# Row factors of a graph attention: by DMA through DRAM instead of by transposes on PE

## The reference

```python
h = jnp.einsum('bmi,ih->bmh', x, Wp) + bp
scores = s_src[:, :, None] + s_dst[:, None, :]
scores = jnp.where(scores >= 0, scores, 0.2 * scores)
attn = jax.nn.softmax(jnp.where((A_final <= 0)[None], fill, scores), axis=-1)
h_gat = jnp.einsum('bmn,bnh->bmh', attn * A_final[None], h)
```

## Time and profile before

| | us |
|---|---|
| median of 2 runs | 1026.09 (1020.98 to 1031.19) |
| the profiled execution | 1025.88 |
| its span in the profile | 1024.1 |

### The profile page before, as it was taken

One profiled execution on the slowest core, in us unless ns is written; L12 is line 12 of the kernel. 1 busy time (PEld: TensorE's weight loads), 2 busy tenths in 40 slices (PEclk: granted clock), 3 DMA queues, 4 the chain that ended last, 5 costly groups with the idle time before them and its releaser, 6 DMA issues. The chain is left out here.

```text
span 1024.1 us, 21202 instructions
## 1 busy us (share of the span) xinstructions
PE 957.3 (93%) x7355; PEld 908.4 (89%) x7355; DVE 870.2 (85%) x2532; ACT 632.7 (62%) x1641; POOL 549.4 (54%) x1169
## 2 busy tenths in 40 slices
PE   6779999999999999999999999999999899997998
PEld 5679998998988899899989899999899899887897
DVE  5989797999989987978899889699989879779884
ACT  2446557686668653675575674777548584777741
POOL 3426254681786651755566464456727635467831
PEclk9878999999999998999999999999999999999999
DMA  7020000000020010002000101100000100000004
GB/s 141 2 62 2 1 2 1 2 2 1 2 83 2 2 42 2 1 21 63 2 1 1 43 1 42 43 2 22 22 1 2 42 2 2 1 1 2 1 1 124
DMA packets 38490, 20.17 MB, mean 20 GB/s; under 512 B 3184, under 2 KB 37872, under 8 KB 38384
## 3 DMA queue, kind: packets, MB, share of 16 engines
q1 hardware_dynamic: 36512, 18.42, 6.8%
q10 hardware_dynamic: 1872, 0.40, 0.2%
HBM read 10.43 MB, written 8.39 MB: 18 GB/s over the span
## 5 line engine op out<-in xcount | busy, mean ns | idle before, releaser
L639 PE MATMUL ps<-HE,PT 128*128 128x129 f32 x2048 | 241.0, 277 | 5.9 <-issue 2.3
L639 PEld LDWEIGHTS ps<-HE,PT 128*128 128x128 f32 x2048 | 234.8, 193 | 9.3 <-issue 8.6
L925 ACT ACTIVATE Y<-X,SM 128x128 f32<-128x128 f32 x512 | 203.9, 487 | 41.8 <-POOL SM L1083 41.7
L1068 POOL TENSOR_TENSOR SM<-ST 128x8 f32<-128x8 f32 x96 | 28.4, 296 | 294.9 <-DVE ST L1154 294.8
L1291 DVE SCALAR_TENSOR_TENSOR PT<-ps,CE,maskT 128x512 f32<-128x512 f32 x256 | 174.1, 742 | 13.7 <-PE ps L763 7.8
L1079 POOL TENSOR_TENSOR SM<-SM,minus_half 128x8 f32<-128x8 f32 x96 | 162.1, 1688 | 7.6
L639 PE MATMUL ps<-W,HT 128*128 128x128 f32 (+1 forms) x768 | 126.7, 312 | 0.7 <-issue 0.4
L639 PEld LDWEIGHTS ps<-W,HT 128*128 128x128 f32 x768 | 116.0, 193 | 10.1 <-ACT HT L918 0.6
L1154 DVE BATCH_NORM_STATS2 ST<-X 128x6 f32<-128x128 f32 x512 | 104.9, 277 | 3.2
L656 PE MATMUL ps<-ident,Y 128*128 128x128 f32 x640 | 86.5, 279 | 11.5 <-ACT Y L925 9.8
L656 PEld LDWEIGHTS ps<-ident,Y 128*128 128x128 f32 x640 | 72.5, 144 | 17.7 <-ACT Y L925 15.4
(11 more groups left out here) (262 smaller groups left out, 2348.9 us busy)
## 6 DMA issues: line engine op xcount, KB each, us to landing
X<-in_x_dram SPq DMA_DIRECT2D x32, 256.0 KB, 3.4
out_dram<-X SPq DMA_DIRECT2D x32, 256.0 KB, 2.8
adj_raw<-in_adj_dram SPq DMA_DIRECT2D x4, 256.0 KB, 3.7
W<-in_L_gnn_W_dram SPq DMA_DIRECT2D x1, 128.0 KB, 5.7
Ws<-n_L_gnn_self_weight_dram ACTq DMA_DIRECT2D x1, 64.0 KB, 3.1
W<-in_L_gnn_W_dram ACTq DMA_DIRECT2D x1, 64.0 KB, 3.5
feat2w<-in_L_gnn_W_dram ACTq DMA_DIRECT2D x1, 64.0 KB, 4.3
Wo<-L_gnn_others_weight_dram SPq DMA_DIRECT2D x1, 64.0 KB, 5.8
```

Source lines behind the costliest of these rows:

```text
L639: return nc.tensor.matmul(o, w, m, start=start, stop=stop, skip_group_check=True)
L925: a = A(dst[:, n, 0:F], src[:, n, 0:F], func, scale=SM[s][:, S_RSTD, n:n + 1], bias=SM[s][:, S_SHIFT, n:n + 1])
L1068: TT(sm[:, S_DIF, :], st[:, :, 1], st[:, :, 4], ALU.subtract)
```

## The change

1. The four steps `spread1a`, `spread1b`, `spread2a`, `spread2b` of PE go. In their place come `spill1`, `fill1`, `spill2`, `fill2` on SP: two DMAs write `CE`'s columns 8 to 15 (512 elements of 4 bytes each DMA) to a scratch in DRAM, and one DMA reads the 1024 factors back, 4 KB to each of the 128 partitions, into `HI[s]`. `fill` waits for the landing of `spill`.
2. The DVE step of the attention reads the row factors from `HI[s]` in SBUF instead of from PSUM, waits for `filled` instead of for the PSUM tile, and no longer waits for its own end.
3. The set-up block: `erank` (16 matmuls of 128 x 512 and four copies) moves from the edge work into it; 32 small matmuls with `cnt_row` give way to four that turn `off_b`; row counts come from ACT's accumulator instead of two DVE reductions; some copies go from DVE to ACT; loads are cut into three sets, with fewer broadcasts; for groups 0 and 1 (`EARLY`) the first layer norm's statistics, `rstd` and scaling are done there.
4. `TURNS` and `HOMES` are written anew, for all engines and all steps.

```diff
+EARLY = 2
-    ("spread1a", 1, "pe"),
-    ("spread1b", 1, "pe"),
+    ("spill1", 0, "sp"),
+    ("fill1", 0, "sp"),
...
 PREP = [
-    ("erank", 4, "pe act"),
...
+                def spill(u, name, s):
+                    n = ATT[name[-1]]
+                    sp.wait_ge(sig["dexp"][s], count(u.g, 4, 2 * n))
+                    for b in range(G):
+                        sp.dma_start(factors[s, n, b * N:(b + 1) * N].rearrange("(t p) -> p t", p=P),
+                                     CE[s][:, TG + b:2 * TG:G],
+                                     allow_slow_non_contiguous=True).then_inc(sig["spilled"][s], 16)
+
+                def fill(u, name, s):
+                    n = ATT[name[-1]]
+                    sp.wait_ge(sig["spilled"][s], count(u.g, 2, n) * 16 * G)
+                    sp.dma_start(HI[s][:].bitcast(F32).rearrange("p r f -> p (r f)"),
+                                 factors[s, n, :].partition_broadcast(P)).then_inc(sig["filled"][s], 16)
...
-                def spread(u, name, s, b):
-
-                    pe.wait_ge(sig["dexp"][s], count(u.g, 4, 2 * ATT[name[6]]))
-                    o, done = open_tile(u, name, s)
-                    for t in range(T):
-                        n = TG + t * G + b
-                        mm = T_(o[:, t * P:(t + 1) * P], wide(CE[s][:, n:n + 1]), ident[:])
-                    mm.then_inc(done, 1)
...
-                    o, read = filled(u, "spread" + name[3:], s)
+                    dve.wait_ge(sig["filled"][s], count(u.g, 2, n) * 16)
+                    o = HI[s][:].bitcast(F32).rearrange("p r f -> p (r f)")[:, b * N:(b + 1) * N]
                     for j in range(T):
                         c = j * G + b
                         a = V.scalar_tensor_tensor(out=PT[r][:, j, :], in0=o, scalar=CE[s][:, c:c + 1],
                                                    in1=maskT[:, j, :].bitcast(F32), op0=ALU.max, op1=ALU.mult)
                     a.then_inc(p_full[r], 1)
-                    dve.wait_ge(p_full[r], u.matrix(name)[1] + 1)
-                    dve.sem_inc(read, 1)
```

In the set-up block:

```diff
+                for i in range(T):
+                    for j in range(T):
+                        mm = MM(ps[i // 2][:, (i % 2) * N:(i % 2 + 1) * N], maskT[:, j, i * P:(i + 1) * P],
+                                upper[:, j, :], start=(j == 0), stop=(j == T - 1))
+                    if i % 2 == 1:
+                        mm.then_inc(made["rank"], 1)
...
+                for s in range(EARLY):
+                    if s == 1:
+                        act.wait_ge(made["rowtot"], 1)
+                        A(rowtot_b[:], ps[3][:, 0:N], ACT.Copy)
+                        for h in range(2):
+                            act.wait_ge(made["rank"], h + 1)
+                            A(rank[:, 2 * h:2 * h + 2, :], ps[h][:].rearrange("p (a n) -> p a n", a=2), ACT.Copy)
+                    act.wait_ge(sig["rstd"][s], 1)
+                    scaled(Y[s], X[s], s, ACT.Relu).then_inc(sig["normed"][s], 1)
```

More of the change, by code:

```diff
@@ L446, in _ @@
                     sp.sem_inc(s, 16)
[L447 removed]
+                sp.wait_ge(loaded["rest"], 16 * len(REST))
             @block.gpsimd
@@ L467, in _, with link @@
                 nc.gpsimd.iota(mc_int[:], [[P, MB]], base=0, channel_multiplier=1).then_inc(made["pool"], 1)
+                order = [0]
+                def link(ins):
+                    order[0] += 1
+                    ins.then_inc(pool_order, 1)
+                    pool.wait_ge(pool_order, order[0])
+                for s in range(EARLY):
+                    pool.wait_ge(sig["var"][s], 1)
+                    rstd_of(pool, link, s, False).then_inc(sig["rstd"][s], 1)
+                pool.wait_ge(loaded["rest"], 16 * len(REST))
+                nc.gpsimd.tensor_scalar(bias3[:], bias3[:], -1.0, None, ALU.add)
+                pool.sem_clear(pool_order)
             @block.tensor
@@ L506, in _ @@
                 MM(ps[2][:, 390:391], bprep[:], asum[:], start=True, stop=True).then_inc(made["wvec"], 1)
+                for i in range(T):
[4 more added lines that the diff above has]
+                        mm.then_inc(made["rank"], 1)
+                pe.wait_ge(made["off_b"], 1)
+                for i in range(T):
+                    mm = MM(ps[2][:, N + 400 + i:N + 401 + i], off_b[:, i * P:(i + 1) * P], ident[:, 0:1], start=True, stop=True)
+                mm.then_inc(made["off_col"], 1)
             @block.scalar
@@ L628, in store @@
                         sp.dma_start(rows_of(out, u, b), X[s][:, b::G, :]).then_inc(sig["stored"][s], 16)
-                walk("sp", {"load": load, "store": store})
+                def spill(u, name, s):
[10 more added lines that the diff above has]
+                                 factors[s, n, :].partition_broadcast(P)).then_inc(sig["filled"][s], 16)
+                walk("sp", {"load": load, "store": store,
+                            "spill1": lambda u, s: spill(u, "spill1", s), "fill1": lambda u, s: fill(u, "fill1", s),
+                            "spill2": lambda u, s: spill(u, "spill2", s), "fill2": lambda u, s: fill(u, "fill2", s)})
                 for s in range(NS):
@@ L810, in mlp @@
                         mm.then_inc(done, 1)
-                def erank(u, s):
-                    for i in range(T):
-                        o, done = open_tile(u, "erank", s, i)
-                        for j in range(T):
-                            mm = MM(o, maskT[:, j, i * P:(i + 1) * P], upper[:, j, :], j == 0, j == T - 1)
-                        mm.then_inc(done, 1)
                 def eoffm(u, s):
@@ L828, in eedge @@
                 def eedge(u, s):
-                    for i in range(T):
-                        turned(u, "erank", s, i)
                     for t, src in enumerate((adjn, rank)):
@@ L999, in feat3 @@
                         A(HI[s][:, t * G:(t + 1) * G, :], v[:, :, F:2 * F], ACT.Copy).then_inc(sig["hi"][s], 1)
-                def erank(u, s):
-                    for i in range(T):
-                        o, read = filled(u, "erank", s, i)
-                        A(rank[:, i, :], o, ACT.Copy).then_inc(read, 1)
                 def eedge(u, s):
```

349 lines of the change are left out of this document (176 added, 173 removed).

## The result

The changed kernel takes **1283.44 us** (median of 2 runs, 1281.79 to 1285.1) where the kernel before takes 1026.09: a ratio of 1.254 [1.247, 1.261], 257 us slower. The profiled execution took 1281.8 us, with a span of 1279.7.

A forecast was written before the change was run, and what follows sets the result against it. The prediction took PE's amount of work as the bound, DVE second with 14% slack. From 1025.9 us it took 28.2 for transposes and 9 for set-up, added 12 for collisions and 2 for DMAs: 1003 us, range 984 to 1032.

The forecast's parts named there:

- transposes gone: PE's 256 transposes removed: 64 sets at 0.44 us, 28.2 us saved, upper bound 38.4.
- PE's amount of work sets the time: Once the groups run, PE is the bound; work taken from it is worth nearly its full price.
- The spill's price: Attention's round trip through DRAM: 3.25 us for the spills' landing, 3.9 for the fill, together 7.2 us.
- The lead, about 9 us: Steps between `dexp` and first attention step: 4.9 steps, 10.3 us, less about 1 for ACT's exponentials; most fills in time.
- rival of late DMAs: Spill to fill of 10 us or more delays at least half of 32 attentions by 2 to 3 us: 1031 us; chance 0.15.
- if DVE's first idle reason is the fill: Sign that the prediction is wrong: DVE idles mostly for fills, where 10 to 30 us of such idling was expected.
- The port: Attention instructions with two SBUF inputs and wide POOL ones exclude each other: DVE loses 30 us, PE 12, bounds 3 and 50.
- I take 0.4: Share of DVE's 30 us of collision loss that reaches PE, giving 12 us; the trace suggested a third.
- Four of five delays left no idle PE: Of five collision delays in the earlier trace, 6 us, only one showed as idle PE; argued that DVE's slack hides them.
- the port decides: Rival: DVE, held by POOL, becomes the bound; all 50 us reach PE plus 10 from narrow instructions: 1049, middle 1030; chance 0.16.
- The new order: Rewritten order of steps on all engines: left at zero, give or take some 8 us of PE's idle time.
- The set-up and start: `erank` hidden in set-up 6.3, shorter set-up 1, less PE idle before 112 us 2: saves 9 us, bounds 4 and 14.

The follow-up runs named there:

- e16: Kernel before, old order, without the transposes; DVE's attention line replaced by an equally long maximum over 576 elements of one SBUF input; 1020.88 us, 0.998.
- e17: Changed kernel's order and set-up without spill and fill; DVE's attention line replaced by a maximum over 576 elements of one SBUF input; 1071.85 us, 1.047.
- e1: Changed kernel without spills and fills; DVE's attention line reads a block of maskT in SBUF in place of the row factors; 1095.87 us.
- e12: Changed kernel with the spill's 1024 4-byte pieces written 64 B apart to another scratch, the fill reading a fixed dense block; 1095.56 us.
- e18: Kernel before, transposes and waits kept, only the attention line's first input moved from PSUM to SBUF; run four times; 1091.43 us, 1.065.
- e8: Kernel before with one transpose in place of four in each set, 192 of 256 gone; 1023.83 us, 0.998.
- e13: Kernel before with eight transposes in place of four in each set, 256 more; 1035.36 us, 1.014.
- e2: Changed kernel with one spill of 128 pieces of 32 B in place of two of 512 4-byte pieces; DVE reads at a stride of eight; 1183.68 us.
- e4: Kernel before, transposes and waits kept, only the attention line's first input moved from PSUM to SBUF; one run; 1091.36 us.
- e10: Kernel before with the attention line's first input in SBUF and three of POOL's four wide lines cut to 128x8 elements; 1043.27 us, 1.017.
- e9: Kernel before with three of POOL's four wide lines cut to 128x8 elements, 48 of 64 wide instructions; 1021.05 us, 0.995.
- e7: Kernel before with only the changed kernel's set-up block, old attention through PE and old order kept; 1023.09 us, 1.003.
- e14: Kernel before with DVE's attention line working on 256 of 512 columns; 1017.85 us, 0.994.
- e15: Kernel before with DVE's attention line on 256 of 512 columns and one transpose per set in place of four; 1014.37 us, 0.992.
- e3: Kernel before, old order and set-up, without the 256 transposes, and with both inputs of DVE's attention line in SBUF; 1088.71 us.

## Why the prediction was wrong

The measured medians put the way from before to after in steps. (They add up to 261, since the kernel before took 1022.5 us beside e16 and e17, not 1026.1.) e1 and e12 ran once each, so the 24 of the third link is good to some us only. That link depends on the order: it is +69 us in the old one (e18).

| step | from, to | us | forecast |
| --- | --- | --- | --- |
| transposes gone | before 1022.5, e16 1020.9 | -2 | -28 |
| new order and set-up | e16, e17 1071.9 | +51 | -9 |
| both inputs in SBUF | e17, e1 1095.9 | +24 | +12 |
| DMAs that come late | e1 or e12, after 1283.4 | +188 | +2 |

**"PE's amount of work sets the time" failed first**, before any of the new costs. It was read from a busy share of 93% and from a chain whose last 68 us are PE alone. Both are true, and neither says that work taken from PE comes back as time. e8 and e16 took it and PE was idle instead. Taking 63 us of DVE's work gave 7, and taking both gave 11 us. No engine's amount of work alone is the limit. What remains is the order by hand, in which every engine runs a fixed list and waits across engines fill what a shorter step leaves; that reading is by exclusion, and which waits they are was not followed. The asymmetry of e13 and e8 (+10 against about 0) fits it. The mean granted clock was higher with more transposes and lower with fewer: 0.983 in e13, 0.974 before, 0.967 in e16, and 0.961 in e8, where PE's busy time fell by only 11.8 us for 192 transposes.

**The spill's price failed by the most.** The step was "I take 7.2": 3.25 us for the landing of the spills, read off a pair of stores of 256 KB, and 3.9 for the fill. The fill was nearly right, 3.7 us in e12 and 4.9 in the kernel after. The spill was not: 9.8 us from issue to fill at 107.90, 13.2 at 716.76, some 10 of it waiting. The whole way is about 16 us, over twice the forecast. The row chosen had the same number of pieces, but not 4-byte ones that lie side by side, and e12 shows that this is what counts. The lead, about 9 us, held: in e12, where no fill holds DVE up, the attention starts 8.7 us after the spill's issue (median of 32), and in the kernel after 16.4. 16 - 9 = 7 us late, and 6.1 us of waiting are measured. Even the upper price in the text, 10 us, was too low. The rule of the Trainium skill, "DMA: Bandwidth & Descriptors", section "Specifications", that pieces under 512 B are written by read-modify-write, pointed to the right side; but e12's 4-byte pieces and e2's 32-byte pieces are under 512 B as well and were waited for 1.6 and 1.4 us, so the rule alone doesn't give the price, and no run here shows the read-modify-write itself.

**The rival of late DMAs was the right mechanism** (0.15, 1031 us, "decides from about 9 us on"), with a delay of 2 to 3 us for half of the attentions. The delay was 6.1 us for 29 of 32, and more than all of it reached the end: 178.0 us of waiting on DVE, 188 us of time. PE's idle time rose from 133.3 (e12) to 279.7 us, by 146, and its busy time by 39.5 at a clock of 0.886 against 0.936. The prediction's own sign of being wrong, "if DVE's first idle reason is the fill", named it.

**The port: cause and size on DVE right, its way to PE wrong.** The attention line's median stayed (747 ns in e4, 744 after), the maximum is over 2.5 us (2886), the mean of 911 lies in the range of 800 to 950. 43 us of loss stand against 30 forecast and an upper bound of 50. But "I take 0.4" of it for PE failed: PE's idle time rose by 44.7 us where DVE's busy time rose by 44.5, as if all of it had reached PE, and PE's busy time took 20.8 more at the lower clock. "Four of five delays left no idle PE" was counted on single delays in other lines; the attention line's stand directly in front of PE's matmuls, as at 567.98 in e4. And POOL's own chains are longer too, which the sum put at nothing beyond the step from 0.33 to 0.4; e10 shows PE idle 16.5 us more with hardly any loss on DVE. e18's +69 us is what the rival "the port decides" had (60 over its base). In the new order the same address cost 24 us (197.4 us for the line in e12, mean 835); it meets POOL less there, (835 - 742) x 256 = 24 us against 43. In the kernel after itself the mean is 756. So the forecast "mean of 800 to 950" failed there, and not because the port was harmless; that the wait for the fill leaves the line little chance to meet POOL is the likely reason, not shown.

The Trainium skill, "SBUF — State Buffer", section "Who interferes with whom", has a DVE instruction with two SBUF inputs contend with every GpSimd instruction that reads SBUF. The runs agree for wide instructions, and for narrow ones in one direction: in e10, 152 of 157 waited for DVE. In the other direction they don't: none of 163 attention instructions that started inside a narrow one was held, as in the earlier trace rows. As to the price, e9 and e10 put some 48 of 70 us on three wide lines, 106 us of POOL's busy time, and some 22 on all the rest, over 400 us of it.

**The new order had "no price in rows"** and was left at zero, give or take 8. It costs 51 us in e17 with no spills and fills, no transposes and no second SBUF operand, while e7 shows the set-up innocent. PE's busy time rises there by 15.9 (clock 0.967 to 0.952) and its idle time by 34.4. Why this order is worse stays open: its `HOMES`, its turns on all engines and its distance of 5.9 places between `top` and attention changed together, and no run parts them.

**The set-up and start.** Right: the second block begins with transposes, and as early as said. From the kernel after in order of time, against the earlier trace rows:

```profile
28.89 3.65 PE L736 MATMUL ps<-ident,Y 128*128 128x128 f32 x16 [6.57 <-ACTq L457]
```

Wrong: that this is worth 9 us. From 29.8 to 112 us PE is idle 14.3 us against 9.0, and e7 moves nothing: PE's busy time is 10.9 us shorter there (946.4), and its idle time 8.2 longer.

The other signs that the prediction named: PE's busy time at 925 (927.7 in e16, where only the transposes are gone; 1000.0 after, at the lower clock); PE idle 50 to 60 us from 112 on (244.2).

No run gives a version that clearly beats the kernel before. Keeping the order and the PSUM operand is within 0.3% of it (e7), and the cuts of e9, e14 and e15 leave work out for under 1%. What the new kernel would take with a quick spill is e12's 1095.6 us; its fill does not read the pieces that were written apart, and a kernel that does was not run. Moving POOL's wide work to another engine was not tried either.

## What to carry to other kernels

A busy share of 93% and a chain that ends on an engine don't show that its work is the bound: before pricing what a change takes away, ask for the idle time that would come in its place, and try the removal by itself if that is possible. A round trip through DRAM must be priced by rows with its own layout, not by bytes or piece counts, and set against its lead in the issuing engines' order; here, where it was late, the 178 us of waiting counted in full. And where an operand of a frequent DVE instruction moves from PSUM to SBUF, count POOL's wide instructions beside it: here that one address cost 6.5% in the old order.

## What the runs showed of the hardware

- **4-byte pieces side by side in DRAM land slowly.** 512 or 1024 of them made the fill wait 10 us, the same 1024 pieces 64 B apart 1.6 us, 128 pieces of 32 B side by side 1.4 us. The last packet record of a pair begins 1.8 us after the issue in the slow case (after) as in the quick one (e12). Why the landing is late was not shown.
- **A stride costs DVE.** The attention line with its first input at a stride of eight fp32 elements took 1145 ns at the median (e2), dense 744.
- **Narrow POOL instructions wait for a DVE instruction with two SBUF inputs, and don't hold it.** In e10, 152 of the 157 that started beside the attention line were held, 60 us in all; none of the 163 attention instructions that started beside a narrow one was. With one input in PSUM (e9) none of 243 was held.
- **The granted clock was lower in the kernels in which PE idled more**, though not strictly. With PE's idle time in us: 0.983 (e13, 57.7), 0.974 (before, 66.8), 0.967 (e16, 90.4), 0.948 (e4, 111.5), 0.936 (e12, 133.3), 0.913 (e2, 192.5), 0.886 (after, 279.7). Out of line are e10 (0.975, 78.7), e17 (0.952, 124.8) and e3 (0.951, 132.2). The matmuls that read `PT` took 309 ns at the mean after, 277 before. From e12 to the kernel after, with the same number of matmuls, PE's busy time rose by 39.5 of the 188 us.
